# One core, four chained layers: VectorE's order at the turn of a block, and TensorE's order behind the last block

## The reference, cut to what matters

```python
x = x + L0(x, ...)   # scores from tanh(x W1 + b1) v, masked softmax by row type, weighted sum of tokens
x = x + L1(x, ...)   # attention, 16 heads of 8, bias per row from u_prev, out @ Wo.T + bo
x = x + L2(x, ...)   # h = relu(x wi.T + low-rank terms); out = h wo.T + low-rank terms
                     #   low rank: a common pair, and one of 8 experts chosen by the row's id
x = x + L3(x, ...)   # h = gelu(x fc1.T + b); 96 outputs from fc2, 32 from one of 16 experts by the row's id
```

## Time and profile before

| | |
|---|---|
| runs, us | 259.78 median of 3 (258.68 to 262.64) |
| the profiled execution, us | 258.46, of which the span from its first to its last instruction is 256.7 |
| busy in the span | TensorE 245.5 us, VectorE 187.5, ScalarE 137.7, GpSimd 121.7 |
| granted TensorE clock | 1.000 of 2.4 GHz |

### The profile page before, as it was taken

The page is one execution under the profiler, slowest core; times in us unless marked ns, Lnnn a source line. Parts: engine busy times, 40 slices in busy tenths (PEclk is TensorE's granted clock), DMA queues, the critical chain, the costliest instruction groups (busy, mean ns, idle before and its releaser), DMA issues.

```text
span 256.7 us, 12675 instructions
## 1 busy us (share of the span) xinstructions
PE 245.5 (96%) x4862; PEld 183.9 (72%) x4862; DVE 187.5 (73%) x349; ACT 137.7 (54%) x253; POOL 121.7 (47%) x242
## 2 busy tenths in 40 slices
PE   7999999897999999999999999999999999889993
PEld 5666455676687858787778767786878587758983
DVE  4879887886878787887888787878787868563041
ACT  3175455672819653774648382858196528541250
POOL 5876612653515461645345443536154445464240
PEclk9999999999999999999999999999999999999999
DMA  6978403550455225530654055503554541255011
GB/s 182 369 238 244 137 3 125 222 208 31 127 206 208 86 76 213 204 123 6 239 204 163 0 200 200 214 0 132 200 205 189 211 169 43 84 222 193 3 43 43
DMA packets 27326, 38.27 MB, mean 149 GB/s; under 512 B 10769, under 2 KB 11537, under 8 KB 27170
## 3 DMA queue, kind: packets, MB, share of 16 engines
q1 hardware_dynamic: 26578, 36.99, 40.3%
q10 hardware_dynamic: 720, 0.89, 1.2%
HBM read 10.60 MB, written 2.10 MB: 49 GB/s over the span
## 4 chain that ended last, share of the span: by engine, by line
PE 82%; SPq 5%; DVE 5%; DMA 3%; ACT 2%; issue 2%; ACTq 0%; DVEq 0%
PE pB L786 11%; PE pB L869 9%; PE pB L739 7%; PE pB L743 6%; PE pooled L714 6%; PE pB L740 6%; PE pooled L682 5%; PE pV L729 4%; PE pooled L676 3%; PE pV L694 3%; SPq L277 2%; PE pV L735 2%; SPq L276 2%; PE pB L846 2%; PE pB L821 2%
## 5 line engine op out<-in xcount | busy, mean ns | idle before, releaser
L403 POOL COPY rw<-e3t_s 128x128 f32 x128 | 40.5, 317 | 54.6 <-issue 50.0
L382 POOL TENSOR_TENSOR sc<-sc,rmax 128x512 f32<-128x512 f32 x32 | 33.7, 1052 | 42.5 <-DVE rmax L1166 42.4
L507 ACT ACTIVATE ex<-sc 128x512 f32<-128x512 f32 x32 | 20.2, 630 | 27.3 <-POOL sc L382 26.9
L786 PE MATMUL pB<-rwo,hid 128*32 128x128 f32 x1024 | 33.3, 275 | 1.4 <-DMA rwo<-weff 1.3
L786 PEld LDWEIGHTS pB<-rwo,hid 128*32 128x32 f32 x1024 | 26.7, 109 | 5.1 <-issue 2.6
L1161 DVE SCALAR_TENSOR_TENSOR sc<-pooled,bias 128x512 f32<-128x512 f32 x32 | 21.7, 678 | 11.6 <-PE pooled L714 9.7
L413 POOL COPY rwo<-weff 128x512 f32 x32 | 21.4, 674 | 16.9 <-ACT weff L528 5.8
L1172 DVE STREAM_TRANSPOSE pt<-ex 128x512 f32<-128x512 f32 x32 | 22.4, 700 | 6.5 <-ACT ex L507 6.5
L511 ACT ACTIVATE hid<-pB 128x512 f32<-128x512 f32 x32 | 18.3, 594 | 12.0 <-PE pB L743 11.7
L869 PE MATMUL pB<-rw,hT 128*32 128x128 f32 x768 | 24.4, 274 | 0.0
L1166 DVE TENSOR_REDUCE rmax<-sc 128x16 f32<-128x512 f32 x32 | 22.0, 686 | 1.1
(11 more groups left out here) (181 smaller groups left out, 521.1 us busy)
## 6 DMA issues: line engine op xcount, KB each, us to landing
rwo<-weff SPq DMA_DIRECT2D x96, 256.0 KB, 2.3
rw<-fc2t_dram SPq DMA_DIRECT2D x4, 768.0 KB, 12.3
xT<-xt_dram SPq DMA_DIRECT2D x7, 256.0 KB, 2.7
xN<-xn_dram SPq DMA_DIRECT2D x7, 256.0 KB, 2.9
out_dram<-o_s SPq DMA_DIRECT2D x7, 256.0 KB, 2.3
e3t_s<-e3t_dram SPq DMA_DIRECT2D x1, 1024.0 KB, 10.5
rwo<-ffn_w_dram SPq DMA_DIRECT2D x1, 896.0 KB, 6.4
rwo<-ffn_w_dram SPq DMA_DIRECT2D x1, 512.0 KB, 12.0
```

The lines of the kernel that those rows point to most:

```text
L382: pool.tensor_tensor(sc[:, g % 2, :, :], sc[:, g % 2, :, :], rmax[:, g % 2, :].unsqueeze(2).to_broadcast([P, H, S]), ALU.subtract).then_in ...
L403: pool.tensor_copy(rw[:, r, :, SHARED:D], e3t_s[:, bass.ds(e, 1), :, :].rearrange("p o c n -> p (o c) n"))\
L786: last = mm(pB2[S * q:S * q + S, P * g:P * g + P], hid[:, c, tok], rwo[:, Q4 * g + q, c, :], start=(c == 0), stop=(c == FC - 1))
```

## The change

In every block VectorE's `x3` is cut in two: `x3_high(n-1)` (high part and x3T), then `x2(n)`, then `x3_low(n-1)`. `x2(n)` now waits for x3T, because x3T is made from the x2 that it writes over. Behind the last step TensorE's order is another: `hidden(7, 1)` stands right behind `low(7)` and writes bank pA1 in place of pB2; `final(6, 2)` stands behind `out_rows(7)` and `final(6, 3)` behind `out_turn(7)`; the two filling matmuls are gone. ScalarE's relu of chunk 1 reads pA1 there.

```diff
+        HID_END = [pB1, pA1, pB0, pB1]
@@ scalar
-                relu(NBLK - 1, c)
+                relu(NBLK - 1, c, HID_END)
@@ tensor
-                if c == 1:
+                if c == 1 and banks is HID:
                     at(pe, res_sb, ...)
@@ tensor, behind the last step
             low(NBLK - 1)
+            hidden(NBLK - 1, 1, HID_END)
             final(NBLK - 2, 0, pA0)
             final(NBLK - 2, 1, pA0)
-            for c in range(FC):
+            hidden(NBLK - 1, 0)
+            hidden_expert(NBLK - 1, 0)
+            hidden_expert(NBLK - 1, 1, HID_END)
+            for c in range(2, FC):
                 hidden(NBLK - 1, c)
                 hidden_expert(NBLK - 1, c)
+            out_rows(NBLK - 1, *range(G))
             final(NBLK - 2, 2, pA0)
-            out_rows(NBLK - 1, *range(G))
+            out_turn(NBLK - 1)
             final(NBLK - 2, 3, pA0)
-            out_turn(NBLK - 1)
             token_major(NBLK - 2, pA1)
-            keep_busy(2, pS0, ffn_p[0])
             fc1(NBLK - 1)
             token_major(NBLK - 1, pB0)
             final_by_chunk(NBLK - 1)
@@ vector
             def x2(i):
                 at(dve, wo_ps, i + 1)
+                at(dve, x3_sb, i)
@@ vector, step_of
-                x3(n - 1)
+                x3_high(n - 1)
                 x2(n)
+                x3_low(n - 1)
```

More of the change, by code:

```diff
@@ L174, in cond_resid_kernel @@
         pS = [pS0, pS1]
+        HID = [pB1, pB2, pB0, pB1]
+        HID_END = [pB1, pA1, pB0, pB1]
         GIN = [pB1, pB2, pS0, pS1]
@@ L507, in exps, with relu @@
                 act.activation(ex[:, g % 2, :, :], sc[:, g % 2, :, :], ACT.Exp).then_inc(ex_sb, 1)
-            def relu(i, c):
+            def relu(i, c, banks=HID):
                 at(act, hid_ps, FC * i + c + 1)
-                act.activation(hid[:, c, :], [pB1, pB2, pB0, pB1][c][:, :], ACT.Relu).then_inc(hid_sb, 1)
+                act.activation(hid[:, c, :], banks[c][:, :], ACT.Relu).then_inc(hid_sb, 1)
             def gelu(i, c):
@@ L752, in whole @@
                 return [w[:, :] for w in pair]
-            HID = [pB1, pB2, pB0, pB1]
             def low(i):
@@ L759, in low, with hidden @@
                 parts3(pB0[:, :], weight(N_EIA), whole(x2p), True, True, (x2l_sb, i + 1)).then_inc(low_ps, 1)
-            def hidden(i, c):
-                if c == 1:
+            def hidden(i, c, banks=HID):
+                if c == 1 and banks is HID:
                     at(pe, res_sb, i - 1 if isinstance(i, int) and i == NBLK - 1 else i)
@@ L769, in hidden, with hidden_expert @@
                     at(pe, hid_sb, FC * i + 1)
-                parts3(HID[c][:, :], weight(N_I, c), whole(x2p), True, False)
-            def hidden_expert(i, c):
+                parts3(banks[c][:, :], weight(N_I, c), whole(x2p), True, False)
+            def hidden_expert(i, c, banks=HID):
                 at(pe, low_sb, 2 * (i + 1))
-                parts3(HID[c][:, :], weight(N_EIB, c), whole(lowp), False, True, (lowl_sb, i + 1)).then_inc(hid_ps, 1)
+                parts3(banks[c][:, :], weight(N_EIB, c), whole(lowp), False, True, (lowl_sb, i + 1)).then_inc(hid_ps, 1)
             def out_rows(i, *groups):
@@ L1211, in mask_low, with x3_high @@
                 tt(lowp[1][:, :], lowm[:, :], lowp[0][:, :], ALU.subtract).then_inc(lowl_sb, 1)
-            def x3(i):
+            def x3_high(i):
                 at(dve, outT_ps, i + 1)
@@ L1216, in x3, with x3_low @@
                 tt(x3T[:, :], pB0[:, :], x2T[:, :], ALU.add).then_inc(x3_sb, 1)
+            def x3_low(i):
                 at(dve, x3_sb, i + 1)
@@ L1310, in _ @@
             mask_low(NBLK - 1)
-            x3(NBLK - 1)
+            x3_high(NBLK - 1)
+            x3_low(NBLK - 1)
             dve.wait_ge(row_ps, G)
```

## The result

The changed kernel takes 263.29 us (median of 4 runs, 262.32 to 265.37); before, in the same sessions, 259.23 us. The ratio is 1.0189, 95% interval 1.0138 to 1.0239: slower by 4.9 us, and by 3.6 to 6.2 us with the interval. One run of before, 262.64 us, was in a slower state that every kernel shows now and then, and this and all later ratios leave such runs out (without it the median of before is 258.68 us, which is why the ratio says more than the 4.1 us between the two medians). The mean granted clock of the changed kernel's four runs was 1.000, 1.000, 0.984 and 0.993, at 262.54, 262.32, 265.37 and 264.04 us. The profiled execution is the one of 262.54 us, with a span of 260.8 against 256.7 and full clock to its last matmul, so the trace explains 4.1 us, which lies inside the interval.

A forecast was written before the change was run, and what follows sets the result against it. TensorE was taken to bound the loop, busy 27.31 of 27.31 us. Loop +2.3 and tail +1.2 make +3.5 us: 262.0 on the profiled execution's 258.46, 263.3 on the median, forecast 263.2, range 260.0 to 265.6.

The forecast's parts named there:

- the two terms: The loop's six turns, +2.3 us, and the tail behind the last step, +1.2 us: together +3.5 us.
- The wait for x3's low part: At each block turn, TensorE's line 850 waits for the later low part: 0.59 us lost, bounds 0.54 to 0.67.
- VectorE's gap: At each turn, x2 standing ahead on VectorE puts x3's low part 0.66 us later.
- Line 743's old loss: TensorE's wait for x2's low part at block turns, 1.21 us over six, would go.
- rival 3: In the loop, line 743 keeps its loss, x2's low part being held behind biased_x3: 1.2 us more, 264.5; chance 0.10.
- The last turn: Behind the last turn, final(6, 0) waits for the gelus and starts at about 231.1 against 231.06: no change.
- The tail: Behind the last step, fc1 ends 0.83 us earlier but token_major(7) waits for GpSimd: +1.2 us, 1.05 to 1.35.
- Rival 1: In the tail, GpSimd doesn't gate the end: tail -0.83 us, sum +1.5, 261.3; chance 0.15.
- rival 2: In the loop, line 850's 0.59 us is absorbed by later TensorE waits: 259.0, or 261 with tail +1.2; chance 0.12.
- rival 4: TensorE's clock falls in the idle time ahead of token_major(7): 3.5 us more, 266.7; chance 0.05.

The follow-up runs named there:

- e1: Kernel before with only x2 put ahead of x3's low part on VectorE, TensorE's old order at the end: ratio 1.0107 to before.
- e3: e1 with x3's low part moved behind x1 too: ratio 1.0292 to the kernel before.
- e6: e1 with fc1 issuing its fourth chunk's two high-part matmuls ahead of its wait for x3's low part: ratio 1.0069 to the kernel before.
- e9: e6 with GpSimd's biased_x3 waiting for x2's low part: ratio 1.0011 to the kernel before.
- e4: e2 with the last four copies of block 7's expert weights made by VectorE instead of GpSimd: ratio 1.0008 to the kernel before.
- e5: e2, but final(6, 2) stays ahead of out_rows(7) and final(6, 3) ahead of out_turn(7): ratio 0.9982 to the kernel before.
- e7: e2 with biased_x3 behind part 2, then the last four expert-weight copies shared, two on GpSimd and two on VectorE: ratio 0.9991 to before.
- e2: Kernel before with only TensorE's new order at the end and its fillers gone, VectorE's old order: ratio 1.0109 to before.
- e10: The changed kernel with seven unused filling matmuls between fc1(7) and token_major(7): ratio 1.0159 to the kernel before.
- e8: e2 with seven unused filling matmuls between fc1(7) and token_major(7): ratio 1.0034 to the kernel before.

## Why the prediction held

The direction and both mechanisms were right, and each of the two terms came out 0.2 to 0.35 us above its forecast. Step by step:

- *The wait for x3's low part.* Forecast 0.59 us a turn, measured 0.68. VectorE's gap was the mis-sized term: the low part ends 0.74 later, not 0.66, because x2 starts 0.11 behind x3T (92.10 to 92.21), where the low part started 0.04 behind it (200.27 to 200.31). Why is not shown: both have two waits in front of them. So 0.68 lies just above the bounds of 0.54 to 0.67 a turn. Net 2.65 us for six turns against 2.3, inside the bounds 2.0 to 3.5; 6 x 0.68 - 1.21 would be 2.87, so some 0.2 us came back elsewhere in the blocks. e1 and e3 show the place of the low part as the cause.
- *Line 743's old loss goes, by a hair.* Right: no wait there in the changed kernel, with x2's low part held to 1.26 us as forecast, at five turns of seven. e6 shows how near that was, e9 what held it. So rival 3 was a real mechanism that here had no price.
- *The last turn changes next to nothing.* `final(6, 0)` starts 5.91 us behind the turn (228.37 to 234.28), before 5.80; forecast 0.04 more.
- *The tail.* Forecast +1.2 (1.05 to 1.35), measured +1.40, of which 0.11 is the item above and 0.1 is `out_rows`. `biased_x3` ended 6.84 us behind `final(6, 2)` (252.75 and 245.91 in the chain); forecast 6.73 to 7.03. TensorE's idle time was 1.99 us, forecast 1.65 to 1.9. Rival 1 (GpSimd doesn't gate) is refuted by that wait, and by e4, e5 and e7, where it is gone.
- *The loss is absorbed in the block* (rival 2): refuted, the turns are 0.44 us further apart.
- *The clock* (rival 4, given 0.05): underrated. It isn't in the profiled execution, but it is in e2's trace behind the same idle time, at 1.6 us, not 3.5, as the clock came back within the last layer. It may be why the measured ratio, 4.9 us, is above the traces' 4.1, and e10, with that idle time filled, is at 1.0159 x 258.65 - 258.65 = 4.1; the changed kernel's two runs at full clock took 262.54 and 262.32 us, the two at a lower mean clock 264.04 and 265.37. None of this shows it, since the intervals take in 4.1 and 4.9 alike. Whether it fell there in the changed kernel at all stays open.

So the near agreement of 263.2 and 263.29 is partly luck: the two terms were 0.55 us too small together, and the median of before came out 0.55 lower. For the profiled execution 262.0 was the sum, and 262.54 came.

## What to carry to other kernels

Before an instruction is moved ahead of another on a strict queue, look when the one that is put back is needed: here it was wanted 0.05 us after it was done, and the wait that the move took away was a third as long as the one that it made. A reorder on one engine also moves the start of whatever its results release, here eight copies on an engine that had been working in the shade of a long stretch. And behind the same idle stretch on TensorE the clock fell in one trace (e2) and not in another (the changed kernel), and e8, with that stretch filled, ran 0.75% under e2: fillers that look useless in one trace may be worth their place.

## What the runs showed of the hardware

VectorE's low part of x2 (128 x 512, float32) took 0.68 us alone and 1.25 us when it started 0.35 us behind GpSimd's `biased_x3` (e6); with `biased_x3` behind it, it took 0.68 again (e9). GpSimd's copy of one expert's weights costs 0.67 us in a row, of which 0.30 is the copy; on VectorE the same copy took 0.23 us in the shortest case, but in a row, with its index loaded, 0.75 (245.64 to 247.88 for three steps in e4).
